# A two-layer MetaFormer block on one Trainium2 core: the first attention's queries, keys and relative terms computed per block between heads, its values product turned round, and the max scores five heads ahead

## The reference, cut to what matters

```python
win = xp.reshape(B, nwh, ws, nww, ws, C).transpose(0, 1, 3, 2, 4, 5)
win = win.reshape(B * nwh * nww, ws, ws, C)          # ws = 14, N = 196
qkv = win.reshape(Bw, N, C) @ qkv_w.T + qkv_b        # 12 heads of 16 channels
attn = jnp.einsum('bnd,bmd->bnm', q * scale, k)
rel_h = jnp.einsum('bhwc,hkc->bhwk', rq, Rh)
rel_w = jnp.einsum('bhwc,wkc->bhwk', rq, Rw)
attn = (attn.reshape(-1, ws, ws, ws, ws) + rel_h[:, :, :, :, None] + rel_w[:, :, :, None, :]).reshape(-1, N, N)
attn = jax.nn.softmax(attn, axis=-1)
out = attn @ v
out = out @ proj_w.T + proj_b
```

## Time and profile before

| | |
|---|---|
| median of 3 runs | 1086.57 us (1085.85 to 1089.51) |
| the profiled execution's own time | 1082.64 us |
| its span | 1080.8 us |
| mean granted TensorE clock | 0.847 |
| TensorE busy | 782.3 us (72%) |
| TensorE's weight loads busy | 664.9 us (62%) |
| VectorE busy | 564.3 us (52%) |
| GpSimd busy | 441.6 us (41%) |
| ScalarE busy | 326.1 us (30%) |

### The profile page before, as it was taken

One profiled execution on the slowest core, in us unless ns is written; L12 is line 12 of the kernel. 1 busy time (PEld: TensorE's weight loads), 2 busy tenths in 40 slices (PEclk: granted clock), 3 DMA queues, 4 the chain that ended last, 5 costly groups with the idle time before them and its releaser, 6 DMA issues.

```text
span 1080.8 us, 18138 instructions
## 1 busy us (share of the span) xinstructions
PE 782.3 (72%) x5320; PEld 664.9 (62%) x5321; DVE 564.3 (52%) x1124; ACT 326.1 (30%) x718; POOL 441.6 (41%) x737
## 2 busy tenths in 40 slices
PE   4980699898989726999999256044448269999991
PEld 2470598787889416999999134011126159999991
DVE  5233667576674564333332540999955653333324
ACT  1752354244433212333333032000003123333330
POOL 0203342321320124666665331367711246666651
PEclk9965599899899766999999676578978669999996
DMA  8144443333220381111111317930019301111115
GB/s 225 32 152 124 75 86 63 58 68 68 39 36 2 108 349 29 48 48 46 50 51 37 116 47 151 183 57 19 19 36 386 114 29 50 48 46 50 48 37 175
DMA packets 65265, 92.06 MB, mean 85 GB/s; under 512 B 23380, under 2 KB 47028, under 8 KB 64504
## 3 DMA queue, kind: packets, MB, share of 16 engines
q1 hardware_dynamic: 55176, 69.24, 24.8%
q0 software_dynamic: 10048, 22.31, 7.0%
HBM read 66.98 MB, written 25.81 MB: 86 GB/s over the span
## 4 chain that ended last, share of the span: by engine, by line
PE 53%; DVE 27%; DMA 7%; issue 6%; POOL 3%; ACT 2%; SPq 2%; DVEq 0%; POOLq 0%; ACTq 0%
PE ps L1054 12%; PE ps L1062 9%; PE ps L1066 6%; PE ps L639 5%; DVE rt L1335 4%; PE ps L1592 2%; PE ps L644 2%; DVE qq L483 2%; DVE x_sb L1001 2%; DVE xn L1328 2%; DVE arena L1328 2%; DMA qd<-arena 2%; PE ps L1045 2%; PE ps L1395 2%; PE ps L295 2%
## 5 line engine op out<-in xcount | busy, mean ns | idle before, releaser
L1108 ACT ACTIVATE arena<-ps,b1s 128x128 f32<-128x128 f32 x468 | 129.5, 375 | 213.3 <-PE ps L1066 133.7
L1054 PE MATMUL ps<-arena 128*128 x936 | 165.4, 327 | 1.5 <-DVE rt L969 1.5
L1054 PEld LDWEIGHTS ps<-arena 128*128 128x128 f32 x936 | 150.3, 190 | 2.4 <-issue 2.1
L433 POOL TENSOR_TENSOR kk<-arena,kk 16x1536 fp32r<-16x1536 f32 x16 | 64.7, 4041 | 142.6 <-ACT kk L744 142.5
L1062 PE MATMUL ps<-xnT 128*128 128x128 f32 x936 | 120.1, 279 | 2.3 <-DVE xnT L962 2.3
L1062 PEld LDWEIGHTS ps<-xnT 128*128 128x128 f32 x936 | 116.8, 195 | 3.7 <-DVE xnT L962 3.7
L1405 PE MATMUL ps<-xnT,cst 128*128 128x512 f32 (+3 forms) x88 | 45.1, 644 | 66.0 <-POOL xnT L1287 66.0
L1120 POOL TENSOR_TENSOR credit<-credit 1x1 f32<-1x1 f32 x306 | 56.9, 186 | 79.8 <-DVE rt L969 35.4
L1287 POOL TENSOR_TENSOR xnT<-arena,rt 128x1024 f32<-128x1024 f32 (+3 forms) x21 | 65.5, 3144 | 50.2 <-DVE rt L1362 38.0
L1128 POOL DMA_INDIRECT xnT<-xnd,gcur x78 | 78.6, 1008 | 15.7 <-issue 14.7
L639 PE MATMUL ps<-arena 98*102 98x196 f32 x384 | 80.4, 357 | 0.0
(11 more groups left out here) (197 smaller groups left out, 1413.8 us busy)
## 6 DMA issues: line engine op xcount, KB each, us to landing
arena<-in_w SPq DMA_DIRECT2D x16, 576.0 KB, 10.4
arena<-in_w1a SPq DMA_DIRECT2D x16, 384.0 KB, 10.6
arena<-yd SPq DMA_DIRECT2D x8, 768.0 KB, 7.2
arena<-kd SPq DMA_DIRECT2D x48, 96.0 KB, 5.8
arena<-qd SPq DMA_DIRECT2D x16, 264.0 KB
arena<-qd SPq DMA_DIRECT2D x16, 192.0 KB
arena<-in_w1b SPq DMA_DIRECT2D x16, 192.0 KB, 10.9
qkvd<-arena SPq DMA_DIRECT2D x32, 96.0 KB
```

Source lines behind the costliest of these rows:

```text
L433: nc.gpsimd.tensor_tensor(dst, fk[cc % 2][R_DUP:R_DUP + HD], dst.bitcast(F32), ALU.subtract)\
L1054: last = mm(ps[:, DOWN, 0:C], hidT[r][:, f, :], w2s[:, e, f, :], start=f == 0, stop=f == FT - 1)
L1108: last = nc.scalar.activation(hidT[r][:, f, :], hidden(r, f), ACT.Gelu, bias=b1s[l][:, bass.ds(e * FT + f, 1)])
```

## The change

The first attention is written anew. The experts and the second attention stay, but for the order of the tokens.

- **Token order.** The host gives x, and takes the output, with the tokens of each block in the order of the windows. `permute` and GpSimd's `window_order` go. Where the second attention needs the natural order, `ln_copy` (for its layer norm) and the copies into yT take three pieces per 96 x 512 half, and the copies were one piece before.
- **One front per block.** A front is: transposes of the normed tokens (x0, x1), three query and key products of 128 columns (t0, t2, t1: eight heads' queries, eight heads' keys, and the other four of both), the relative terms (r0, r1 for eight heads, 32 records of 32 moving columns each; r2 for four heads), and the values (v0, v1). The front of block 0 stands ahead of the heads, with a PSUM bank for each part. Those of blocks 1 to 3 stand between the heads of the block before, at heads 0 to 4, 7 and 8, in MISC.
- **High and low parts.** ScalarE writes a plain and a rounded copy of each product (`round_heads`), GpSimd subtracts, and GpSimd itself issues the stores into qd and kd (16 per block). The loads go straight from DRAM into q0 and k0; fq, fk, `round_q`, `round_k`, `q_low` and `k_low` go.
- **Values product.** The exponentials are the weights (98 or 120 columns) and the values of one head move (17 columns: 16 channels and a one for the sum). The result has queries on the partitions. `normalise` takes reciprocals of it and multiplies, `transposed_outputs` turns it on TensorE, `copy_outputs` (ScalarE) takes it out. The buffers of exponentials are three in place of two.
- **Bias.** The projection's bias is a row of ones in ot and a row in wp; GpSimd's addition of it goes.
- **Padding keys** are made on the chip from a small table, with no trip to DRAM.
- **Max scores** run AHEAD = 5 heads ahead. The max transposes of a chunk stand at the second head of the chunk before.
- The loops over blocks are written out in full.

The values product, and GpSimd's part of a front:

```diff
-                for i in range(2):
-                    for c in range(2):
-                        mm(ps[0:VW, PV, i * WA:(i + 1) * WA], v0[0:WAH, g, 2 * i + c, at],
-                           x[0:WAH, i, c * WA:(c + 1) * WA], start=first, stop=False, skip_group_check=True)
...
+                for i in range(2):
+                    for c in range(2):
+                        for kc in range(2):
+                            mm(o[0:WAH, 2 * i + c, hh], x[0:WAH, i, kc * WA + c * WAH:kc * WA + (c + 1) * WAH],
+                               v_[0:WAH, 2 * i + kc, h], start=(hh, i, c, kc) == (0, 0, 0, 0), stop=False,
+                               skip_group_check=True)
...
+            def heads_split(kind, b):
+                m = int(kind[1])
+                pool.wait_ge(s_("act_emptied"), EMPTIED[kind, b])
+                if m < 2:
+                    rows = P if m == 0 else P // 2
+                    for o, s in zip(natural_pieces(qf[0:rows, m]), window_pieces(src_w[0:rows, m])):
+                        last = nc.gpsimd.tensor_copy(o, s)
+                    last.then_inc(s_("qf_ready"), 1)
+                nc.gpsimd.tensor_tensor(src_lo[:, m], src_w[:, m], src_hi[:, m].bitcast(F32), ALU.subtract)\
+                    .then_inc(s_("split"), 1)
+                pool.wait_ge(s_("split"), split_at(kind, b))
+                store(kind, b)
...
+            for b in range(BLKS):
+                heads_split("t0", b)
+                heads_split("t2", b)
+                rel_split("r0", b)
+                rel_split("r1", b)
+                heads_split("t1", b)
+                rel_split("r2", b)
```

More of the change, by code:

```diff
@@ L108, in build @@
         wv0 = sb("wv0", [KC, 2, C])
[L109 to L110 removed]
+        wp = [sb(f"wp{l}", [KC + 1, 2, C]) for l in range(2)]
+        bp1 = sb("bp1", [P, C])
         bv0 = sb("bv0", [P, C])
@@ L192, in build @@
[L192 to L201, removed]
+        src_hi = ar(0, [3, BT]).bitcast(F32R)
+        src_lo = ar(3 * BT, [3, BT]).bitcast(F32R)
@@ L361, in peeled @@
[L361 to L366, removed]
-        def attn0_sync(sp):
[L369 to L416, removed]
@@ new lines, in residual @@
+            def residual(b, half):
+                v.wait_ge(s_("misc_full"), FULL[f"p{half}", b])
+                xs = x_sb[:, b * TPB + 2 * half:b * TPB + 2 * half + 2, :]
+                nc.vector.tensor_tensor(xs, xs, ps[:, MISC, 0:2 * C].rearrange("p (t c) -> p t c", t=2), ALU.add)\
+                    .then_inc(s_("dve_emptied"), 1)
+            for g in range(2):
+                values(0, g)
+            for H in range(AHEAD):
+                maxima(H)
+                if H == HC - 1:
+                    minus(0)
@@ L580, in attn0_vector @@
[L580 to L594 removed]
+                    for kc in range(2):
+                        last = mm(ps[0:rows, bank_of(f"v{g}", b), k * KC:(k + 1) * KC],
+                                  xnTb[b % 2][:, kc, k * WAH:k * WAH + rows],
+                                  wv0[:, kc, g * KC:(g + 1) * KC], start=kc == 0, stop=kc == 1)
@@ new lines, in attn0_tensor @@
+            for k in range(2):
+                transposes(0, k)
+            pe.wait_ge(s_("wqk_ready"), 3)
+            queries_and_keys(0, 0)
+            queries_and_keys(0, 2)
+            pe.wait_ge(s_("rel_in"), 32)
+            relative(0, 0)
+            relative(0, 1)
+            queries_and_keys(0, 1)
+            relative(0, 2)
+            pe.wait_ge(s_("small_in"), 16 * 13)
+            for g in range(2):
+                values(0, g)
+            pe.wait_ge(s_("act_emptied"), EMPTIED["r2", 0])
@@ L1719, in layout @@
         o[f"b2_{l}"] = rows(i[n[3]])
+    tok, img = tok[:BT] % PIX, tok[:BT] // PIX
     y, x = np.divmod(np.arange(PIX), SIDE)
[L1723 to L1726 removed]
     win = (y // WS * 2 + x // WS)[tok]
```

934 lines of the change are left out of this document (477 added, 457 removed).

## The result

The changed kernel takes **1235.4 us** (median of 4 runs, 1229.36 to 1279.75) where the kernel before takes 1088.04 (1085.85 to 1090.64): a ratio of 1.1337, 95% interval 1.127 to 1.1403. It is slower by 13%.

The account below looks back on a forecast made before the run. TensorE's work plus what stops it bounds the heads. From 1082.6 us: front -65, heads +36, later copies +3, tail -4, unseen waits +4 give 1056.6; with 3.9 for the median, 1060 us. Range 1032 to 1190.

Parts of the forecast that it names:

- the clock falls among the heads: Rival, chance 0.25: heads at half clock, 6.3 us each; 1132 us if a third of the loop, 1204 if two thirds.
- 3.3 us a head: Heads without front work: both score products and a values product of 22 x 0.090 us, at full clock.
- First exponential: Start of the heads: first exponential near 63 us in place of 128.4, 65 us earlier, with only block 0 computed ahead.
- GpSimd: Per block: subtractions of 1.2 us, store issues of 0.8 us, 25 us in all; sets the front's pace, hidden between heads.
- Values product: In each head: 22 records x 0.090 us = 1.98 us, set by weight loads, so no gain over 1.95 us.
- Front work: Between heads, for blocks 1 to 3, on TensorE: transposes, query/key products and relative terms, 16.8 us a block.
- cheaper: Rival, chance 0.08: narrow weight columns of the last relative term side by side and no unseen waits, 1030 us.
- Waits on MISC: TensorE waiting in order on the single MISC bank's uses through ScalarE or VectorE: 5.7 us a block.
- Blocks: Block 0 67.5 us, middle blocks 72 us each (now 60.6), the last 42.5 us to its last exponential.
- Copies in the later stages and the tail: Later stages: ScalarE copies cut into pieces for the token order, 3 us more; tail without reciprocals and spread, 4 us less.
- Five heads ahead at nothing: Max scores five heads ahead, not six: the row lands in 4.6 us of 5.3, just in time, no cost.
- the row of maxima is late: Rival, chance 0.07: row lands late at chunk starts, 15 chunks x 2.7 us, 1100 us; decides once landing exceeds 2.8 us.

Follow-up runs that it names:

- run 3: The changed kernel with eight more matmuls for nothing per head on TensorE (16 weight columns, 152 moving columns each): 1243.04 us, one run.
- run 2: The kernel before with the values product's moving columns cut to 17 in five heads of six, same weights: 1127.12 us, ratio 1.0323.
- run 5: The changed kernel with only the values product turned back (values as weights, exponentials moving) and the spread of reciprocals back: 1091.15 us, ratio 1.0023 to the kernel before.
- run 6: The changed kernel with max scores six heads ahead in place of five: 1233.54 us, ratio 1.1329 to the kernel before.
- 7: The kernel of run 5 with max scores six heads ahead in place of five: 1122.28 us, ratio 1.031 to the kernel before.
- 9: The kernel of run 5 with the first two relative terms each cut in halves among longer work, third query/key product moved: 1096.39 us, ratio 1.0086.
- 11: The kernel of run 5 with one long matmul for nothing ahead of each first two relative terms, blocks 2 and 3: 1097.96 us, ratio 1.0094.
- 12: The kernel of run 5 with three long matmuls for nothing ahead of each first two relative terms, blocks 2 and 3: 1091.83 us, ratio 1.005.

## Why the prediction was wrong

**The verdict** was the other way: 1060 us and faster, against 1235. The case that came true is the rival *the clock falls among the heads*, at 0.25, with its mechanism and price a head right (6.3 us, measured 6.24), its place right as far as it went (heads 9 to 11 and the last block are at half clock throughout) and its share wrong: I priced a third and two thirds of the loop, it was 94%. By its own rate 94% would be 204 us and 1264 in all, too much: apart from 48 heads of 6.24 us the stage took 119 us, against 105 in my sum at full clock. The rest did not double, among other things because waits do not and because the narrow relative term took 3.6 us at half clock (in the front of block 0), not 7.6. The range, which took the clock case in only to 1190, missed for that alone.

**The step that failed** is "3.3 us a head", the 22 x 0.090 us of the values product at full clock. The 1.98 us are right at that level (1.96 in run 3). What failed is the clock for which they were taken. My argument for full clock was that the new loop has no long wait, and that waits stood ahead of the half-clock stretches before. That reading of the kernel before holds (TensorE waited 2.0 to 2.3 us ahead of six of its half-clock stretches), but waits are not the only way down. The new loop has next to no waits, 97% busy, and run 2 shows that this does not save it: the same loop of before, with the moving columns cut and not a wait added, falls from 0.91 to 0.57. The rows against me were there: the earlier trace rows had 9.28 busy us of 9.60 at 0.50, and the sum itself said that TensorE spends 2 of 3.3 us on loads of weights.

The Trainium skill ("TensorE: Matmul & The Clock Gate", Part 1) has sustained activity release the throttle. By that rule, read as I did, an engine that never pauses keeps its clock, and the result would be 1060. This case's runs disagree for activity with so few moving columns: 97% busy for 419 us, at 0.53.

The terms, one by one, against the earlier trace rows and the runs:

- *First exponential* at 63 us, measured 77.97: 15 us short. Transposes start at 16.62 and not 12.5, because four VectorE operations on 4 elements took 1.1 to 1.4 us each (last section). The first two query/key products take 6.74 us, or 0.84 a record where run 5 has 0.49 at full clock; the profile's clock column reads 1.00 up to 28 us, and the pace says that it was half for most of them. Two copies of `ck` on ScalarE (L897, 2.75 us) stand at the end of the front, and the queue of SP waits for them before any load; I had only seen the two ahead of the root. And I had no trip back from DRAM at all: six instructions of issue (2.8 us), then 9.07 us for the keys. First max scores at 60.27, not 48. The row of maxima adds 5.32 us.
- *GpSimd* subtractions 1.26 us (1.2), issues 0.62 (0.8): right, and it stays hidden.
- *Values product* 1.98 us: right at full clock; at half clock 3.73, so these records take nearly twice as long (1.9 times), as assumed.
- *Front work* 16.8 us a block: relative terms 3.30 (3.2) and 2.06 (3.8: the narrow ones lie side by side, the *cheaper* rival's guess), query/key products 1.95 (1.9).
- *Waits on MISC* 5.7 us a block: 10.4 us in the whole stage at half clock, 7.3 in run 5 at nearly full clock, so about 2 a block. Over-priced.
- *Blocks* 67.5, 72, 72, 42.5: measured by the first exponentials of each 104.9, 117.6, 120.2 and 76.1 (the last to its last exponential, here counted from its first at 420.65). Run 5, with the clock mostly there, has 66.6, 82.4, 80.7 and 44.1.
- *Copies in the later stages and the tail*: +3 - 4, measured +1.0 with all that lies behind the last exponential. Right within 2 us.
- *Five heads ahead at nothing*: right for this kernel (run 6), for a reason I did not give, and wrong in sign of what matters at full clock. The row of maxima is not what it moves: its transfer took 5.32 us in the front, over the 2.8 from which I had it decide, yet it never kept TensorE waiting between heads (at the start of the last block of run 5 the scores stand 4.5 us behind its issue and do not wait). The rival *the row of maxima is late* was also priced at 2.7 us a chunk where its own terms give 3.0. What the five moves is the first max scores of the next block, against the arrival of their chunk, and there five are 31 us better than six. I had written that the chunk is wanted 39 us into a block and that its stores land at 25; in run 5 it lands 45.4 us into the block, as it is wanted. What I left out is the order of SP's queue: the loads of the next block stand behind the row of maxima of the third chunk, which is issued 33.6 us into the block, and not only behind the stores. SP's timeline in run 5 (the chain has 8.45 us more from the last load of keys to its landing):

```profile
108.37 0.65 SPq L482 DMA_DIRECT2D qq<-nm  x1
109.12 1.63 SPq L475 DMA_DIRECT2D qq<-qd  x4
```

**The sum again with the measured terms**: 15 us of first exponential, 156 us of heads (418.7 against 259 + 4), 2 of the rest and 3 of the distance between median and profiled execution are 176, the whole of 1236 - 1060. Of the 156 the clock is nearly all: run 5, with everything of the change but the product, has heads of 273.9 us, 11 above my 259 + 4.

**What the change is worth without its clock** is what 5 says: the front gains 54 us and the heads lose 51. The front work is not gone, it has moved from ahead of the heads to between them, onto the same engine.

**Open**: which part of a front lets the clock fall in some blocks of the kernel of 5 and not in others (block 0 keeps it there in 5, and loses it for a while in its variants 7, 9, 11 and 12; each is one profiled execution, and that of 5, 1084.79 us, is among the fastest of its ten); and how many moving columns would just keep it. No run here varied them in small steps.

## What to carry to other kernels

On TensorE count two things for a loop, its time and how much of it is columns that move: a product turned so that its weights are wide and its moving side is narrow can cost the same at full clock and take the clock from everything around it. A busy share near 100% at a granted clock of 0.5 is the sign, and the test is cheap: cut the moving columns in the old kernel, leave all else, and see whether the kernel gets slower with less work. And tune how far ahead a stage runs only at the clock that you will have; a wait that long heads hide at half clock comes out when they get short.

## What the runs showed of the hardware that was not expected

- Products bound by their float32 weight loads follow the granted clock. 16 records with 98 weight columns and 17 moving ones take 2.53 us at half clock and 1.33 at full (303.66 to 304.99 in run 3).
- Small VectorE operations beside a GpSimd cast. The first two rows are of VectorE's timeline in the changed kernel, 4 elements a partition while GpSimd runs and 12 a partition later; the last is GpSimd's timeline:

```profile
10.67 1.38 DVE L420 TENSOR_TENSOR rt<-rt 128x4 f32<-128x4 f32 x1
...
25.30 0.17 DVE L418 TENSOR_TENSOR rt<-rt 128x12 f32<-128x12 f32 x1
```

```profile
9.16 5.71 POOL L537 CAST qq<-arena 19x1536 fp32r<-19x1536 f32 x4 [2.98 <-DMA arena<-in_cq]
```

  Eight times as long for a third of the elements, in four operations one after another within the cast (1.09, 1.38, 1.39 and 1.36 us, each about as long as one of the four casts, 1.43; the reciprocal ahead of them took 0.18). It came once more beside a GpSimd subtraction, 1.24 us at 25.50. No run took the cast away, so that it is the cause is argued, not shown.
- The turned-back product leaves a gap. It has 17 weight columns and writes to partitions 0, 32, 64 or 96. In the last block at full clock the six records of 120 rows and the step to the scores behind them take 0.71 us in run 5 (343.28 to 343.99) and 0.54 in the kernel before (340.85 to 341.39, 102 weight columns), with 0.31 against 0.21 us in the step ahead of the product: 0.27 us a head, 13 us in 48 heads, and much of why the plain head takes 3.49 us and not 3.23. The cause was not looked for.
